# Moving the side work of a perceiver loop: three placement tables, a new order of 32 row maxima, and four small products of the last batch

## The chip, the cores and the metric

The kernel runs on one core of a Trainium2 chip. The metric is the device time of one execution in microseconds (us). The kernel before takes 948.94 us (median of 3 runs, 947.06 to 949.42). The profiled execution took 947.89 us, of which 946.2 us lie between its first and its last instruction (its span).

The engines are called by their names and, in rows, by their short forms: TensorE (PE; PEld is its weight load), VectorE (DVE), ScalarE (ACT), GpSimd (POOL), SyncE (SP; SPq rows are DMA instructions that it issues).

## The reference, cut to what matters

There are 16 batches. Each has 64 latent tokens and a context of 1601 tokens of 128 numbers. The first and largest layer is a cross attention with 16 heads; a small self attention and a mixture of experts follow on the 1024 latent tokens.

```python
x = layer_norm(image_embeds, ln1_g, ln1_b)      # 16 x 1601 x 128
l = layer_norm(latents, ln2_g, ln2_b)           # 16 x 64 x 128
q = l @ Wq
kv = concatenate([x, l], axis=1) @ Wkv
k, v = split(kv, 2)
w = einsum('bhqd,bhkd->bhqk', q * scale, k * scale)
w = softmax(w)                                  # over 1601 + 64 keys
out = einsum('bhqk,bhkd->bhqd', w, v) @ Wo
...
lam = exp(sum(lq1 * lk1, -1)) - exp(sum(lq2 * lk2, -1)) + 0.8   # in the self attention
```

## The kernel before, in words

**Slots and units.** The key and value maps are folded into the queries and the output map, so the attention works on the normalised tokens themselves. The loop has one slot per batch b, and a slot has 13 units (u = 0 to 12), one per tile of 128 context tokens; unit 12 holds the rest and the batch's own latents. Every number is kept as a high and a low float16 part, so each product is three matmuls in place of one. In each unit:

- TensorE computes the scores of tile u against 1024 query columns: six matmuls of 512 columns (lines 2142, 2145, 2151) into one half of the PSUM tile `S`. In the same unit it weighs tile u-2: six matmuls of 512 columns (2175, 2178, 2181) into `OA`. Scores of unit u wait for `lo_done` of unit u-2.
- ScalarE takes the exponential twice: as the high part (1859, `exponentials_high`) and in full precision back into `S` (1863, `exponentials_full`).
- VectorE subtracts the two and stores the low part (1539, `low_part`; "low" in the tables).

**Side work.** In the same slot the other steps of the batches around b are done, in the places that three tables give them. `TENSOR[u]` has two lists for TensorE: items ahead of the weighing of unit u, and items behind it. `VECTOR[u]` is VectorE's whole list for unit u. `SCALAR[u]` has three lists: ahead of the high exponential, between the two, and behind. Each engine works strictly in the order so written. The items are:

- `q` 0 to 3: the queries of batch b+1 (TensorE 2072 to 2074, 24 matmuls of 64 columns each; ScalarE copies the high part, 1845; VectorE stores the low part, 1518).
- `m` 0 to 31: the scores of batch b+1 with the high parts only, one block of 128 query columns by 512 (or, for the last column block c = 3, 65 + 64) keys each (2085, 2087, 2088). VectorE takes the row maximum of each block (1527), and at the end the maximum over all (1532). `M_ORDER` says which block comes when. `mt` and `shift` bring these maxima into the queries of b+1.
- `left_scores`, `left_sum`, `left_exp`, `left_low`, `left_turned`, `left_copy`, `left`: one context token that doesn't fit a tile, treated apart.
- `stat` (463, 13 a slot), `combine` (453 to 459) and `norm`: the layer norm of batch b+2. `split` 0 to 3 (1406): VectorE's high part of the tokens of batch b+1 in four groups; GpSimd follows each with the low part (1671).
- `outputs`, `latents`: the results of batch b-1 are copied out of PSUM. GpSimd then adds the denominators into `srow` (522). SyncE brings them into a column, `rcol` (512), VectorE takes the reciprocal (`inverse`, 787 and 789), SyncE writes it to memory and reads it back as `rb`, GpSimd multiplies, and ScalarE (`high`, 1840) and GpSimd split the product. `pj` 0 and 1 are the output projection of batch b-2 (2112 to 2114, 48 matmuls each).

**Two banks.** All side results of TensorE go to two PSUM banks, `WW` 0 and 1, in turn (`bank_of_items`). An item waits until the item before the last one, which used its bank, has been read (`bank_free`). The items `m` 5, `left_turned`, `q` 2, `q` 3, `m` 6, `m` 7 follow each other in this alternation: `q` 2 waits until `m` 5 has been reduced, and `m` 7 until the low part of `q` 3 has been stored.

**SyncE's order.** In each slot SyncE issues in this order, one after the other: the transpose of tiles 0 to 7 of b+1 (487), which waits for `split` 1; the transpose of the other tiles (489), which waits for `split` 3; the transpose of the low parts (491), which waits for GpSimd's last part; two small copies for the left token (498, 499); the load of the tokens of batch b+3, 768 KB and 32.5 KB (384, 386), in slots 0 to 12; then `rcol<-srow` (512), and what follows from it (515, 517), and at last `left_row` (507). All of them go through one queue.

**Last slot.** In slot 15 there is no batch to prepare. There the small weights' lambda of the self attention is computed: `small_weights_lambda` (VectorE 692 to 697), `lambdas_scalar` (ScalarE 706) and `lambdas_vector` (VectorE 701, 702), and TensorE starts the next layer in units 3 to 11.

Of the kernel before, what the change touches and what calls it, by code (L numbers as in the profile page):

```python
# [74 lines left out]
SHORT = [(r, 3) for r in range(8)]
M_ORDER = LONG[0:6]
for _k in range(8):
    M_ORDER += LONG[2 * _k + 6:2 * _k + 8] + SHORT[_k:_k + 1]
M_ORDER += LONG[22:24]
assert sorted(M_ORDER) == sorted(LONG + SHORT)  # L80
# [22 lines left out]
VECTOR = [("stat", "stat", "stat", "stat", "latents", "stat", "left_sum", "low", ("split", 0), ("split", 1), "stat", ("q", 0), ("split", 2), "stat",),  # L103
          ("low",),
          ("stat", "stat", "low", "stat", "left_low", ("split", 3), ("q", 1), ("m", 0), ("m", 1), "stat", ("m", 2), "stat", ("m", 3), "stat",),
          ("low", ("m", 4), ("m", 5),),
          ("combine", "low", ("q", 2), ("q", 3), ("m", 6),),
          ("low", ("m", 7), ("m", 8), "inverse", ("m", 9), ("m", 10),),
          ("low", ("m", 11), ("m", 12), ("m", 13),),
          ("low",),  # L110
          (("m", 14), ("m", 15), ("m", 16), ("m", 17), "low", ("m", 18), ("m", 19), ("m", 20), ("m", 21), ("m", 22),),
          ("low",),
          (("m", 23), ("m", 24), ("m", 25), ("m", 26), "low", ("m", 27), ("m", 28), ("m", 29), ("m", 30), ("m", 31),),
          ("low",),
          ("low",)]

SCALAR = [([], [], ["outputs"]),
          ([], [], [("q", 0)]),
          ([], [], ["projected", "left_exp", ("q", 1)]),
          ([], [], []),  # L120
          ([], [], []),
          (["left_copy"], [("q", 2), ("q", 3)], []),
# [2177 lines left out]
```

## Time and profile before

| what | value |
|---|---|
| median of 3 runs | 948.94 us (947.06 to 949.42) |
| profiled execution | 947.89 us, span 946.2 us |
| TensorE busy | 909.3 us, 96% of the span, 8268 matmuls |
| VectorE busy | 798.4 us, 84% |
| ScalarE busy | 701.2 us, 74% |
| GpSimd busy | 378.3 us, 40% |
| granted TensorE clock, mean | 0.994 |
| TensorE's share of the chain that ended last | 80% (VectorE 14%, ScalarE 3%) |

The busy time of a matmul runs from its start to its modelled end, 0.38 us for 512 columns, while the next one starts 0.215 us later; so TensorE can be called busy though it stands still for up to 0.16 us between two matmuls. Its idle time is therefore read from the starts of neighbouring matmuls in the timeline, not from the busy share.

### The profile page before, as it was taken

Reading aid. Unit: us, or ns where it says so; the run is one execution under the profiler, and the core shown is the slowest. Engines: PE = TensorE matmul, PEld = TensorE weight load, DVE = VectorE, ACT = ScalarE, POOL = GpSimd, SP = SyncE. Lnnn points to the kernel's source line nnn. Section 1 sums busy time; section 2 is a strip of 40 time slices with the busy share of each in tenths; the row PEclk is TensorE's granted clock in tenths of the full one; section 3 lists DMA queues with packets and bytes.
Section 4 is the critical chain, followed back from the end, with each engine's and each line's share of the span. In section 5 each row is a group of like instructions: output and inputs, shape, how many; then the busy total and the mean of one; then the engine's idle time right before and its main releaser. Section 6 shows DMA issues by size and latency. Waiting matters only on the chain.

```text
span 946.2 us, 20541 instructions
## 1 busy us (share of the span) xinstructions
PE 909.3 (96%) x8268; PEld 490.1 (52%) x8268; DVE 798.4 (84%) x1591; ACT 701.2 (74%) x1003; POOL 378.3 (40%) x378
## 2 busy tenths in 40 slices
PE   8679999999999999999999999999999999999996
PEld 5444445555454545454545454545454545566763
DVE  5979898979797979898989898888888786588987
ACT  4767878787878787878787878787879676755544
POOL 6472133343444343434343444343434231335345
PEclk9999999999999999999999999999999999999999
DMA  6402030303040303030303030303020200000000
GB/s 214 81 14 61 7 89 2 94 1 95 1 94 1 92 5 83 13 75 21 74 23 73 23 72 24 74 23 73 23 61 23 38 23 2 23 25 24 2 2 23
DMA packets 74566, 41.96 MB, mean 44 GB/s; under 512 B 62276, under 2 KB 69864, under 8 KB 74472
## 3 DMA queue, kind: packets, MB, share of 16 engines
q1 hardware_dynamic: 74184, 39.60, 16.8%
q8 instruction: 66, 1.08, 0.5%
q10 hardware_dynamic: 288, 1.05, 0.3%
q14 instruction: 28, 0.23, 0.1%
HBM read 25.98 MB, written 0.59 MB: 28 GB/s over the span
## 4 chain that ended last, share of the span: by engine, by line
PE 80%; DVE 14%; ACT 3%; issue 2%; DMA 1%; POOL 1%; POOLq 0%; DVEq 0%; ACTq 0%
PE S L2151 10%; PE S L2142 9%; PE OA L2175 9%; PE OA L2178 9%; PE OA L2181 9%; PE S L2145 9%; PE WW L2085 9%; PE WW L2112 1%; PE WW L2113 1%; DVE amx L803 1%; PE WW L2114 1%; PE WW L2072 1%; PE WW L2073 1%; PE WW L2074 1%; DVE mx L1510 1%
## 5 line engine op out<-in xcount | busy, mean ns | idle before, releaser
L1859 ACT ACTIVATE region<-S,sigma 128x1024 f16<-128x1024 f32 x208 | 231.6, 1113 | 135.9 <-PE S L2151 135.9
L1539 DVE TENSOR_TENSOR region<-S,region 128x1024 f16<-128x1024 f32 x208 | 252.4, 1214 | 42.3 <-ACT S L1863 42.3
L1527 DVE TENSOR_REDUCE mx<-WW 128x1 f32<-128x512 f32 (+1 forms) x480 | 262.7, 583 | 29.7 <-PE WW L2085 22.5
L1863 ACT ACTIVATE S<-S,sigma 128x1024 f32<-128x1024 f32 x208 | 224.4, 1079 | 0.0
L1671 POOL TENSOR_TENSOR xk<-raw,xk 128x508 f16<-128x508 f32 x64 | 63.2, 998 | 167.8 <-DVE xk L1406 167.8
L2142 PE MATMUL S<-region,xT 128*128 128x512 f16 (+1 forms) x416 | 124.5, 380 | 3.3 <-DVE region L1539 2.6
L2085 PE MATMUL WW<-xT,region 128*128 128x512 f16 x360 | 124.7, 380 | 3.0 <-DVE region L1518 2.1
L2175 PE MATMUL OA<-region,xk 128*128 128x512 f16 (+1 forms) x416 | 123.8, 379 | 0.0
L2145 PE MATMUL S<-region,xT 128*128 128x512 f16 (+1 forms) x416 | 123.7, 379 | 0.0
L2151 PE MATMUL S<-region,xT 128*128 128x512 f16 (+1 forms) x416 | 123.7, 379 | 0.0
L2178 PE MATMUL OA<-region,xk 128*128 128x512 f16 (+1 forms) x416 | 123.7, 379 | 0.0
L2181 PE MATMUL OA<-region,xk 128*128 128x512 f16 (+1 forms) x416 | 123.7, 379 | 0.0
L550 POOL TENSOR_TENSOR ew<-region,o_hi 128x1024 f16<-128x1024 f32 (+1 forms) x34 | 68.6, 2020 | 53.6 <-ACT o_hi L1840 53.6
L541 POOL TENSOR_TENSOR region<-region,rb 128x512 f32<-128x512 f32 x32 | 40.6, 1270 | 122.6 <-DMA rb<-inv_dram 122.6
L1797 ACT ACTIVATE raw<-raw,smc 128x128 f32<-128x128 f32 (+1 forms) x187 | 86.2, 486 | 0.0
L2151 PEld LDWEIGHTS S<-region,xT 128*128 128x128 f16 (+1 forms) x416 | 41.1, 99 | 48.6
L2178 PEld LDWEIGHTS OA<-region,xk 128*128 128x128 f16 (+1 forms) x416 | 40.6, 98 | 49.1
L2181 PEld LDWEIGHTS OA<-region,xk 128*128 128x128 f16 (+1 forms) x416 | 40.6, 98 | 49.1
L2145 PEld LDWEIGHTS S<-region,xT 128*128 128x128 f16 (+1 forms) x416 | 41.1, 99 | 46.8
L1660 POOL TENSOR_TENSOR smc<-smc,mhalf 128x13 f32<-128x13 f32 x16 | 39.0, 2434 | 61.8 <-DVE smc L459 61.8
L2085 PEld LDWEIGHTS WW<-xT,region 128*128 128x128 f16 x360 | 34.9, 97 | 54.0 <-DVE region L1518 14.1
L2142 PEld LDWEIGHTS S<-region,xT 128*128 128x128 f16 (+1 forms) x416 | 35.0, 98 | 43.5 <-issue 10.1
(318 smaller groups left out, 1830.2 us busy)
## 6 DMA issues: line engine op xcount, KB each, us to landing
raw<-ctx SPq DMA_DIRECT2D x16, 768.0 KB
rb<-inv_dram SPq DMA_DIRECT2D x16, 512.0 KB, 3.5
xT<-xk SPq DMA_TRANSPOSE x48, 3.1
left_row<-left_pT SPq DMA_DIRECT2D x48, 2.0 KB
raw<-ctx SPq DMA_DIRECT2D x16, 32.5 KB
WO_lo<-L_xattn_Wq ACTq DMA_DIRECT2D x1, 512.0 KB, 3.8
WO_hi<-L_xattn_Wkv ACTq DMA_DIRECT2D x1, 512.0 KB, 4.7
lx<-x SPq DMA_DIRECT2D x1, 512.0 KB, 5.7
```

The lines of the kernel that those rows point to most:

```text
L1527: nc.vector.tensor_reduce(mx[:, r, c:c + 1], W[BANK[("m", n)]][:, 0:width], AX.X, ALU.max)\
L1539: nc.vector.tensor_tensor(p_lo[k], src, p_hi[k], ALU.subtract).then_inc(lo_done.sem, 1)
L1797: ins = nc.scalar.activation(x_[0:r, t, :], x_[0:r, t, :], ACT.Identity, bias=smc[0:r, 2, t:t + 1], scale=smc[0:r, 1, t:t + 1])
L1859: nc.scalar.activation(p_hi[k], src, ACT.Exp, scale=sigma[:, 0:1])
L1863: nc.scalar.activation(src, src, ACT.Exp, scale=sigma[:, 0:1]).then_inc(e_done.sem, 1)
L2085: ins = mm(w, rows, xT_hi[p][:, 512 * c:512 * c + 512], start=True, stop=True)
L2142: mm(banks[r, k, :], hi, q_hi[p][:, cols(qc, k)], start=True, stop=False)
L2145: mm(banks[r, k, :], hi, q_lo[p][:, cols(qc, k)], start=False, stop=False)
L2151: ins = mm(banks[r, k, :], lo, q_hi[p][:, cols(qc, k)], start=False, stop=True)
L2175: mm(dst[k], hi, ph[r, cols[k]], start=first, stop=False)
L2178: mm(dst[k], hi, pl[r, cols[k]], start=False, stop=False)
L2181: ins = mm(dst[k], lo, ph[r, cols[k]], start=False, stop=last)
```

## The change

All three tables are written anew, and with them `M_ORDER`. The functions that carry out an item are the same. In words:

- The left token's steps come earlier: its exponential between the exponentials of unit 1, its low part on VectorE in `VECTOR[0]`.
- `pj` 1 moves from unit 2 to unit 1, and `q` 0 behind `pj` 0.
- ScalarE's `outputs` and several others go between the two exponentials or ahead of them; `high` 0 moves from unit 9 to the end of unit 7.
- On VectorE all four `split`s stand in `VECTOR[0]`, `inverse` moves from unit 5 to unit 3, `combine` from unit 4 to unit 5, and the maxima are spread in another way.
- The first parity of the bank alternation is turned (`(n + 1) % 2`).
- In the last slot lambda's steps move from units 0 to 2 to units 7 to 10 (`LAMBDA_AT = 7`).

```diff
-LONG = [(r, c) for c in range(3) for r in range(8)]
...
+M_ORDER = [(0, 0), (3, 0), (4, 0), (2, 0), (5, 0), (0, 1), (3, 1), (6, 0),
+           (0, 2), (2, 1), (7, 0), (4, 3), (6, 1), (3, 2), (6, 3), (4, 1),
...
-        ([("left_scores", 0), ("q", 0), ("pj", 0)], []),
-        ([("pj", 1), ("q", 1)], some(0, 1)),
-        (some(1, 1), some(2, 2)),
+        ([], [("left_scores", 0), ("pj", 0), ("q", 0), ("pj", 1)]),
+        ([("q", 1)], some(0, 1)),
+        (some(1, 2), some(3, 1)),
...
-          ("low", ("m", 7), ("m", 8), "inverse", ("m", 9), ("m", 10),),
+          ("stat", ("m", 1), ("m", 2), "stat", "low", ("m", 3), ("m", 4), "inverse", ("m", 5),),
...
-LEFT_AT = 9
+LEFT_AT = 8
...
-    banks = {item: n % 2 for n, item in enumerate(order)}
+    banks = {item: (n + 1) % 2 for n, item in enumerate(order)}
...
-                    if b is LAST and u == 0:
+                    if b is LAST and u == LAMBDA_AT:
                         small_weights_lambda(dve, link)
-                    if b is LAST and u == 2:
+                    if b is LAST and u == LAMBDA_AT + 3:
                         lambdas_vector(dve, link)
...
-                    if r % 4 == 0 and c in (0, 3):
-                        pe.wait_ge(q_hi_done.sem, q_hi_done.upto(turn, r // 4 + (2 if c == 3 else 0)))
...
+                    if k in Q_FIRST:
+                        pe.wait_ge(q_hi_done.sem, q_hi_done.upto(turn, Q_FIRST[k]))
+                    if k in Q_LATENTS:
+                        pe.wait_ge(q_hi_done.sem, q_hi_done.upto(turn, Q_LATENTS[k]))
```

The other lines of the three tables follow the same pattern. What they do to an engine's order is shown at three places. The first is VectorE in units 0 to 2 of a middle slot. `CAST xk<-raw` is a `split` (the one of 65 partitions is `split` 3), `BN_STATS` a `stat`, `region<-WW,region` the low part of queries, `region<-S,region` a `low`, `left_p` the left token's low part. Before:

```order
L1406 CAST xk<-raw 128x4x127
L463 BN_STATS stc<-raw 128x6
L1518 TENSOR_TENSOR region<-WW,region 128x512 [waits q_hi_done]
L1406 CAST xk<-raw 128x4x127
L463 BN_STATS stc<-raw 128x6
L1539 TENSOR_TENSOR region<-S,region 128x1024 [waits e_done]
L463 BN_STATS stc<-raw 128x6 x2
L1539 TENSOR_TENSOR region<-S,region 128x1024 [waits e_done]
L463 BN_STATS stc<-raw 128x6
L1548 TENSOR_TENSOR left_p<-left_e,left_p 128x8 [waits left_exp]
L1406 CAST xk<-raw 65x127
L1518 TENSOR_TENSOR region<-WW,region 128x512 [waits q_hi_done]
```

And now, from `split` 0 on (line numbers are 8 higher here):

```order
L1414 CAST xk<-raw 128x4x127 [waits pv_done,normed]
L1552 TENSOR_REDUCE left_s<-WW 128x8 [waits pe_left_scores]
L1547 TENSOR_TENSOR region<-S,region 128x1024 [waits e_done]
L1556 TENSOR_TENSOR left_p<-left_e,left_p 128x8 [waits left_exp]
L470 BN_STATS stc<-raw 128x6
L1414 CAST xk<-raw 128x4x127 x2
L470 BN_STATS stc<-raw 128x6 x3
L1526 TENSOR_TENSOR region<-WW,region 128x512 [waits q_hi_done]
L1414 CAST xk<-raw 65x127
L1547 TENSOR_TENSOR region<-S,region 128x1024 [waits e_done]
L1526 TENSOR_TENSOR region<-WW,region 128x512 [waits q_hi_done]
```

The last cast stood behind the `low`s of units 1 and 2; now it stands ahead of the `low` of unit 1, with two casts, three `stat`s and the low part of `q` 0 ahead of it.

The second place is VectorE around the reciprocal of the denominators (`rinv<-rcol`), which waits for the DMA of `rcol`. `mx<-WW` is a row maximum. Before, with `q` 2 and 3 at the head, in units 4 to 6:

```order
L1518 TENSOR_TENSOR region<-WW,region 128x512 [waits q_hi_done] x2
L1527 TENSOR_REDUCE mx<-WW 128x1 [waits pe_m]
L1539 TENSOR_TENSOR region<-S,region 128x1024 [waits e_done]
L1527 TENSOR_REDUCE mx<-WW 128x1 [waits pe_m] x2
L787 TENSOR_SCALAR rinv<-rcol 128x8 [waits den_col]
L789 RECIPROCAL rinv<-rinv 128x8 [waits den_scaled]
L1527 TENSOR_REDUCE mx<-WW 128x1 [waits pe_m] x2
```

Now, in units 3 and 4; the first `low` is that of unit 3:

```order
L1535 TENSOR_REDUCE mx<-WW 128x1 [waits pe_m] x2
L470 BN_STATS stc<-raw 65x6
L1547 TENSOR_TENSOR region<-S,region 128x1024 [waits e_done]
L1535 TENSOR_REDUCE mx<-WW 128x1 [waits pe_m] x2
L795 TENSOR_SCALAR rinv<-rcol 128x8 [waits den_col]
L797 RECIPROCAL rinv<-rinv 128x8 [waits den_scaled]
L1535 TENSOR_REDUCE mx<-WW 128x1 [waits pe_m]
L1547 TENSOR_TENSOR region<-S,region 128x1024 [waits e_done]
L460 TENSOR_TENSOR smc<-stc 128x13 [waits dve_step]
```

The reciprocal moved from behind `q` 2 and 3 and `m` 8 to between `m` 4 and `m` 5.

The third place is TensorE at the end of unit 4 and the start of unit 5, as it is now: `m` 5, the scores of unit 5, `left_turned` and the first matmul of `q` 2.

```order
L2095 MATMUL WW<-xT,region 128x512 [waits m_reduced]
L2152 MATMUL S<-region,xT 128x512 [waits lo_done]
L2152 MATMUL S<-region,xT 128x512
L2155 MATMUL S<-region,xT 128x512 x2
L2161 MATMUL S<-region,xT 128x512 x2
L2110 MATMUL WW<-ident,left_p 128x128 [waits left_low,m_reduced]
L2080 MATMUL WW<-cT_hi,G_hi 128x64 [waits m_reduced]
```

These seven rows are the same in the kernel before, but for the line numbers: on TensorE nothing moved here, and the last `m_reduced` is that of `m` 5 in both. SyncE's and GpSimd's orders are the same in both kernels throughout.

## Rows read from the trace of the kernel before

**Rows 1.** Busy time by stretch, slot 5: length, engines (count), granted clock, DMA

```profile
301.97:349.85 47.88, 47.85 (x430) 24.63 (x429) 41.60 (x81) 38.53 (x53) 19.01 (x17) 1.00 0.19 48
```

**Rows 2.** Timeline of TensorE, slot 5, units 3 and 5: start, length, what

```profile
314.35 0.59 PE L2151 MATMUL S<-region,xT 128*128 128x512 f16 x2
314.94 0.39 PE L2085 MATMUL WW<-xT,region 128*128 128x512 f16 x1
...
319.91 0.59 PE L2142 MATMUL S<-region,xT 128*128 128x512 f16 x2
...
321.26 0.19 PE L2072 MATMUL WW<-cT_hi,G_hi 128*128 128x64 f16 x1
321.29 0.19 PE L2073 MATMUL WW<-cT_lo,G_hi 128*128 128x64 f16 x1
```

**Rows 3.** Timeline of TensorE, slot 5, units 10 and 11

```profile
340.54 0.38 PE L2085 MATMUL WW<-xT,region 128*128 128x512 f16 x1
340.93 0.20 PE L2087 MATMUL WW<-xT,region 128*128 128x65 f16 x1
...
344.23 0.80 PE L2085 MATMUL WW<-xT,region 128*128 128x512 f16 x2
```

**Rows 4.** Timeline of ScalarE, slot 5, unit 0 (in brackets: idle before, releaser)

```profile
303.46 1.11 ACT L1859 ACTIVATE region<-S,sigma 128x1024 f16<-128x1024 f32 x1 [1.39 <-PE S L2151]
304.48 1.08 ACT L1863 ACTIVATE S<-S,sigma 128x1024 f32<-128x1024 f32 x1
```

**Rows 5.** Timeline of VectorE, slot 5, units 0 to 3

```profile
304.87 1.29 DVE L535 COPY region<-WW 128x512 f32<-128x512 f32 x2 [1.72 <-PE WW L2181]
...
306.75 1.21 DVE L1539 TENSOR_TENSOR region<-S,region 128x1024 f16<-128x1024 f32 x1
307.88 0.75 DVE L1406 CAST xk<-raw 128x508 f16<-128x508 f32 x2
...
309.64 1.40 DVE L1406 CAST xk<-raw 128x508 f16<-128x508 f32 x1
...
312.28 0.47 DVE L463 BATCH_NORM_STATS2 stc<-raw 128x6 f32<-128x128 f32 x2
...
314.07 0.21 DVE L1406 CAST xk<-raw 65x127 f16<-65x127 f32 x1
```

**Rows 6.** Timeline of GpSimd, slot 5, the low parts of the tokens

```profile
308.38 2.37 POOL L1671 TENSOR_TENSOR xk<-raw,xk 128x508 f16<-128x508 f32 x2 [8.91 <-DVE xk L1406]
311.12 1.15 POOL L1671 TENSOR_TENSOR xk<-raw,xk 128x508 f16<-128x508 f32 x1 [0.36 <-DVE xk L1406]
```

**Rows 7.** Timeline of SyncE, slot 5: DMA issues

```profile
314.31 1.20 SPq L489 DMA_TRANSPOSE xT<-xk  x1
...
319.55 0.56 SPq L512 DMA_DIRECT2D rcol<-srow  x1
```

**Rows 8.** Line 512 (`rcol<-srow`), all 16 slots: time from issue to landing

```profile
DMA to landing us min/median/max: 2.0/3.9/5.3
```

**Rows 9.** Timeline of VectorE, slot 5, units 4 to 6

```profile
319.60 1.27 DVE L1527 TENSOR_REDUCE mx<-WW 128x1 f32<-128x512 f32 x2
320.79 0.17 DVE L453 TENSOR_TENSOR smc<-stc 128x13 f32<-128x13 f32 x1
...
321.75 1.22 DVE L1539 TENSOR_TENSOR region<-S,region 128x1024 f16<-128x1024 f32 x1
323.22 1.29 DVE L1518 TENSOR_TENSOR region<-WW,region 128x512 f16<-128x512 f32 x2 [0.26 <-ACT region L1845]
...
326.95 0.16 DVE L787 TENSOR_SCALAR rinv<-rcol 128x8 f32<-128x8 f32 x1
327.15 0.20 DVE L789 RECIPROCAL rinv<-rinv 128x8 f32<-128x8 f32 x1
```

**Rows 10.** Timelines of VectorE and TensorE, slot 15 (the last), units 2 and 3

```profile
790.75 1.23 DVE L1539 TENSOR_TENSOR region<-S,region 128x1024 f16<-128x1024 f32 x1 [2.26 <-ACT S L1863]
...
792.03 0.60 PE L2142 MATMUL S<-region,xT 128*128 128x512 f16 x2 [0.91 <-DVE region L1539]
```

More of the change, by code:

```diff
@@ L70, with first_of @@
 MAXIMA = 32
-LONG = [(r, c) for c in range(3) for r in range(8)]
[L75 to L80, printed above, removed]
+M_ORDER = [(0, 0), (3, 0), (4, 0), (2, 0), (5, 0), (0, 1), (3, 1), (6, 0),
[3 rows of a table added]
+assert sorted(M_ORDER) == [(r, c) for r in range(8) for c in range(4)]
+def first_of(test):
+    return [test(r, c) for r, c in M_ORDER].index(True)
+Q_FIRST = {first_of(lambda r, c: r // 4 == k): k for k in range(2)}
+Q_LATENTS = {first_of(lambda r, c: c == 3 and r // 4 == k): 2 + k for k in range(2)}
+XT_FIRST, XT_SECOND = first_of(lambda r, c: c < 2), first_of(lambda r, c: c >= 2)
 def some(first, count):
@@ L101 @@
         ([("mt", 0), ("mt", 1)], [("weigh", 11)])]
-VECTOR = [("stat", "stat", "stat", "stat", "latents", "stat", "left_sum", "low", ("split", 0), ("split", 1), "stat", ("q", 0), ("split", 2), "stat",),
+VECTOR = [("stat", "stat", "stat", "stat", "stat", "latents", "stat", "stat", ("split", 0), "left_sum", "low", "left_low", "stat", ("split", 1), ("split", 2), "stat", "stat", "stat", ("q", 0), ("split", 3),),
           ("low",),
-          ("stat", "stat", "low", "stat", "left_low", ("split", 3), ("q", 1), ("m", 0), ("m", 1), "stat", ("m", 2), "stat", ("m", 3), "stat",),
-          ("low", ("m", 4), ("m", 5),),
-          ("combine", "low", ("q", 2), ("q", 3), ("m", 6),),
-          ("low", ("m", 7), ("m", 8), "inverse", ("m", 9), ("m", 10),),
-          ("low", ("m", 11), ("m", 12), ("m", 13),),
-          ("low",),
[L111 to L114, printed above, removed]
-          ("low",)]
@@ L117 @@
-SCALAR = [([], [], ["outputs"]),
-          ([], [], [("q", 0)]),
-          ([], [], ["projected", "left_exp", ("q", 1)]),
+          (("q", 1), ("m", 0), "low",),
+          ("stat", ("m", 1), ("m", 2), "stat", "low", ("m", 3), ("m", 4), "inverse", ("m", 5),),
+          ("low",),
+          ("combine", ("q", 2), ("q", 3), ("m", 6), ("m", 7), "low", ("m", 8), ("m", 9),),
+          (("m", 10), "low", ("m", 11),),
+          (("m", 12), ("m", 13), ("m", 14), "low", ("m", 15), ("m", 16), ("m", 17), ("m", 18),),
@@ new lines @@
+          ("low", ("m", 19), ("m", 20), ("m", 21),),
+          (("m", 22), "low", ("m", 23), ("m", 24),),
+          (("m", 25), ("m", 26), "low", ("m", 27), ("m", 28), ("m", 29),),
+          (("m", 30), ("m", 31), "low",),
+          ("low",)]
+SCALAR = [([], ["outputs"], []),
+          ([], ["left_exp"], []),
+          ([("q", 0), "projected"], [("q", 1)], []),
+          ([], [], []),
+          ([], [], ["left_copy"]),
+          ([("q", 2), ("q", 3)], [], []),
+          ([], [("norm", 0)], []),
+          ([("norm", 1)], [], [("high", 0)]),
+          ([("norm", 2), ("norm", 3)], [], [("norm", 4), ("norm", 5), ("norm", 6), ("norm", 7), ("norm", 8)]),
@@ L120 @@
           ([], [], []),
           ([], [], []),
[L122 to L130 removed]
+          ([("high", 1), ("norm", 9)], [("norm", 10)], [("norm", 11), ("norm", 12)]),
@@ L1906, in slot @@
                         act.wait_ge(wo_lo_done.sem, WO_GROUPS)
-                    if b is LAST and u == 1:
+                    if b is LAST and u == LAMBDA_AT + 1:
                         lambdas_scalar(act)
```

23 lines of the change are left out of this document (9 added, 14 removed), and 2 rows, old and new, of the table M_ORDER.

## The prediction

> **What bounds the kernel now.** I read the busy time by stretch first, then the timelines of each engine over one middle slot. Slot 5 runs from 301.97 to 349.85; times without a hundreds digit are from its start. It lasts 47.88 us, and TensorE is busy in 47.85 of them at full clock, with VectorE at 41.60, ScalarE at 38.53 [rows 1]. So TensorE bounds the loop, and the sum of matmuls is the same after the change: the most there is to win is TensorE's standing still. I read that from the starts. Two products of 512 columns start 0.21 apart (0.59 less 0.38) [rows 2], so the pair at 314.35 is over at 314.78, and the next starts at 314.94: 0.16 lost in unit 3, where `m` 1 waits for the low part of `q` 1. In unit 10 0.18 go the same way (340.54 and 0.21 against 340.93), and in unit 11 the pair at 344.23 takes 0.80 in place of 0.59 [rows 3]; with its neighbours that unit loses 0.44. Together 0.78 us a slot. All three are waits of a side product for its bank, that is for VectorE. What the tables change is worth 0.78 us at best in a slot, and has no upper limit the other way.
>
> **Units 0 to 4 on TensorE: minus 0.16.** `pj` 1 goes from unit 2 to unit 1 and `q` 0 behind `pj` 0, but the matmuls of units 0 to 4 together stay the same (`m` 0 to 5 in both), so unit 5 starts at 17.94 - 0.16 = 17.78 [rows 2]. The 0.16 go because `q` 1's low part is now first in `VECTOR[2]`, ahead of the `low` of that unit. `scores` of unit 3 needs the `low` of unit 1, which I put at 9.6 to 10.8, and starts at 11.5: covered, by 0.7.
>
> **The four casts, and what follows from the last.** VectorE copies the latents from 2.9 to 4.1 [rows 5]. ScalarE now copies the outputs ahead of its full exponential (each 1.0, an exponential starts 1.5 after the unit [rows 4]), so `low` 0 starts at 5.0 and, with the left token's two small exponentials behind it, `left_low` at 6.5. Then one `stat` (0.2), two casts (0.33 each), three `stat`s and the low part of `q` 0 (0.6) [rows 5, 9]: the last cast is reached at 6.5 + 0.2 + 0.7 + 0.6 + 0.6 = 8.5. GpSimd starts on the second group at 7.2 and does two groups in 2.37 [rows 6], until 9.5. In the trace the cast at 309.64, which begins while GpSimd works, takes 1.40 in place of 0.42 and ends 0.3 behind GpSimd's end at 310.75 [rows 5, 6]. So I take it that the last cast also waits until 9.5 and ends at 9.65; the other bound is 8.7, if it isn't held. Before it ended at 12.31 (314.07 and 0.21) [rows 5].
>
> SyncE's second transpose waits for this cast; `rcol<-srow` is issued 5.27 after the cast's end (319.55 against 314.28), with the transposes, the small copies and the load of the next tokens between, and it is SyncE's own issue time that fills these [rows 7]. GpSimd's `srow` follows the same cast and needs less. So `rcol` is issued at 14.9, 2.7 earlier than now, and lands 3.9 later by the median [rows 8], 4.0 in this slot: at 18.9.
>
> **The reciprocal: plus 0.9 and plus 0.37.** Now it stands in unit 6 at 24.98, when `rcol` has long landed [rows 9]. After the change it comes behind `m` 4 in unit 3's list. Unit 3 starts at 11.5; its exponentials start at 13.0 and 14.0 and end at 15.1 [rows 4]; `low` takes 1.13 until the next instruction [rows 5], `m` 3 and `m` 4 0.6 each [rows 9]: VectorE is there at 17.5, and waits 1.45 for `rcol`. Behind it in the queue are `m` 5, `low` 4, `combine`, the low parts of `q` 2 and 3, and `m` 6.
> TensorE wants `m` 5's bank for `q` 2 at 17.78 + 1.35 = 19.13 (321.26 less 319.91) [rows 2]. With `rcol` at 18.95, 0.33 for the two reciprocal rows and 0.69 + 0.06 for `m` 5 (length and release), `q` 2 starts at 20.03: 0.9 lost.
> A second loss is in the same unit. From `m` 5's start VectorE needs 0.6 + 1.13 (`low`) + 0.96 (`combine`, 320.79 to 321.75) + 0.6 + 0.69 + 0.06 = 4.04 until `q` 3's bank is free [rows 5, 9]. TensorE is ready for it with `m` 7 after 0.75 + 1.4 (`q` 2 and 3, 48 small matmuls at 0.029) + 1.3 (weighing) + 0.22 = 3.67 [rows 2]: 0.37 lost. Without the wait for `rcol`, `m` 5 starts 1.5 earlier and less than 0.1 of it is left.
>
> **Units 6 to 12: plus 0.35, minus 0.62.** By the same lengths every bank of units 6 to 10 is free in time, by 0.2 or more. In unit 11 `low` 10 stands ahead of `m` 27 and 28; the reduction of `m` 28 ends 3.3 after the unit's start, TensorE wants its bank at 3.1, and `m` 31 follows `m` 29 with another 0.15: 0.35 in place of the 0.62 of units 10 and 11 now. `high` 0 at the end of unit 7 (ScalarE, 30) needs GpSimd's product, which is done at about 27: covered by 3, and if it weren't, the exponential of unit 8 would stand behind it.
>
> **A middle slot** then takes 47.88 - 0.78 + 0.9 + 0.37 + 0.35 = 48.72, 0.84 more. The load ahead of `rcol` exists in slots 1 to 12, and the residual's load in its place in slot 13: 13 x 0.84 = +10.9. In slot 0 there is no reciprocal, in slot 14 no load, where `rcol` lands in 2.0 [rows 8] and so ahead of VectorE: there 0.35 is won in each, -0.7.
>
> **The last slot: minus 0.8.** In its unit 3 TensorE starts at 792.03 for want of `low` 1, which had waited 2.26 for ScalarE, and ScalarE for lambda's products [rows 10]: 1.07 lost, and 0.4 ahead of `pj` 0, whose bank is another now. Both go, -1.5. In units 7 and 8 ScalarE's small exponential waits for VectorE's products in the same way, 1.9 behind `low` 7, and holds the exponentials of unit 8 by 2.5. Scores of unit 10 have 1 us of slack on that, but the columns of the first layer's tile, copied behind them, come some 0.7 late for unit 9. Bounds are 0 and 2.5; I take 0.7, since the work behind is for the most part exponentials that have slack.
>
> **Sum.** +10.9 - 0.7 - 0.8 = +9.4 us on the profiled execution's 947.89: 957.3. The median of the runs is 1.05 above that execution, so 958.3.
>
> **Rivals.**
> *Faster: `rcol` is there in time.* It would have to land by 17.5, 2.6 after its issue. The least that the trace has is 2.0 [rows 8], and that speaks for it; the median of 3.9, and the load of 800 KB right ahead of it in the queue, against. Then the 0.9 and all but 0.08 of the 0.37 go: 15 slots x -0.35 = -5.3, with the last slot's -0.8 -6.1, 942.8. Chance 0.20, in which I also put what I may have wrong in VectorE's or SyncE's order of time.
> The Trainium skill (DMA: Bandwidth & Descriptors, on the two cost components) gives a DMA about 2.0 us plus its bytes at 436 GB/s. For 4 KB that is 2.0, which is this rival; line 512's own median of 3.9 doesn't agree, its least value does.
> *No change: the last cast slips in between two of GpSimd's instructions.* It then ends at 8.7, `rcol` lands at 18.0, VectorE waits 0.5 and `q` 2 isn't late, but `m` 7 still is, by 0.38: a slot takes 0.05 less than now, 13 x -0.05 - 0.7 - 0.8 = -2.2, 946.8. For it: the cast comes at 8.5, just behind the change of GpSimd's instructions at 8.4. Against: just behind. Chance 0.12.
> *Much slower: `rcol` lands as late as the longest of the rows, 5.3 after its issue, in most slots* [rows 8], because it and the load now meet the transposes of other data. Then 1.3 more a slot, 13 x 1.3 = 17: 975. For it the spread of the row, against it that the queue's order is the same. Chance 0.08.
> The forecast has 0.60.
>
> **How the numbers follow.** A difference of 0.3% (2.8 us) is about what a measurement of this kernel tells from none. Slower by more: 0.60 + 0.08 = 0.68; within: 0.12; faster: 0.20. The forecast's own range is 953 to 964 (0.4 a slot to either side of the landing, in 13 slots). For 8 in 10 it must reach down through the case of no change into the faster one, to 943, and up to 965; what is left out is the far side of the faster case and the much slower one.
>
> **What would show it.** In the changed kernel's trace: an idle time of VectorE ahead of the reciprocal, 1 to 2 us in slots 1 to 13, put down to the DMA of `rcol`; the start of `q` 2 on TensorE some 20 after the slot's start, behind a gap of about 0.9, and one of 0.4 ahead of `m` 7; the last cast lengthened to over 1 us; a slot of 48.7, but 47.5 for slot 14; no gap in unit 3; units 1 to 3 of the last slot without their 1.5. The prediction is wrong if `rcol` is issued ahead of 13.5 or lands within 2.6, or if VectorE reaches the reciprocal only at 19, since an earlier lateness would then have hidden it.

## The result and the profile after

The kernel after takes 964.19 us (median of 4 runs, 962.66 to 965.80) against 949.18 for the kernel before (4 runs, the three given above among them): a ratio of 1.0151, 95% interval 1.0129 to 1.0173. It is slower, as forecast (958.3, range 943 to 965), but by 15 us in place of 9.4, and only 0.8 below the upper end of that range. The profiled execution took 964.97 us, its span is 963.3.

From here on "middle slots" are slots 1 to 13, and the last slot is measured from its first scores to those of its unit 12. All numbers of this table are starts of TensorE's scores in the profiled executions. Lines of the kernel after are 7 to 10 higher than those of before (VectorE's `low` 1539 is 1547, the row maximum 1527 is 1535, `rcol` 512 is 519).

| stretch, us | before | after | forecast of the difference |
|---|---|---|---|
| ahead of the loop | 62.65 | 62.86 | 0 |
| slots 0 and 14 | 94.7 | 93.4 | -0.7 |
| middle slots | 623.3 | 636.3 | +10.9 |
| last slot, to unit 12 | 40.81 | 44.83 | -0.8 |
| the rest | 124.75 | 125.91 | 0 |

The spans differ by 17.1 where 9.4 were forecast; 4.8 of the 7.7 between them are in the last slot. The page's lines on the engines and on the chain that ended last:

```profile
PE 914.2 (95%) x8268; PEld 495.8 (51%) x8268; DVE 803.8 (83%) x1591; ACT 705.9 (73%) x1003; POOL 378.7 (39%) x378
...
PE 58%; DVE 21%; SPq 7%; DMA 5%; ACT 5%; issue 4%; POOL 0%; POOLq 0%; DVEq 0%; ACTq 0%
```

No engine does other work than before, yet TensorE's share of the chain fell from 80% to 58%. New on it are VectorE's casts, SyncE's issues (7%) and the DMA of `rcol` (5%): the chain from the last cast through the transposes to `rcol` now ends at something that TensorE waits for.

**A middle slot.** Slot 5 now runs from 303.00 to 351.62. Its windows row, with the columns of [rows 1] (length; busy time and count of TensorE, its weight load, VectorE, ScalarE and GpSimd; clock; DMA share; GB/s), answers to that:

```profile
303.00:351.62 48.62, 47.82 (x430) 24.73 (x429) 41.61 (x81) 38.77 (x53) 19.03 (x17) 1.00 0.19 47
```

Nearly the same busy times, full clock, 0.74 longer. Where it goes I follow along the chain, all in slot 5. First VectorE's timeline, units 0 and 4 (in brackets the idle time ahead and its releaser):

```profile
309.64 0.74 DVE L1414 CAST xk<-raw 128x508 f16<-128x508 f32 x2
...
311.47 1.10 DVE L1414 CAST xk<-raw 65x127 f16<-65x127 f32 x1
...
319.28 1.28 DVE L1535 TENSOR_REDUCE mx<-WW 128x1 f32<-128x512 f32 x2
321.83 0.17 DVE L795 TENSOR_SCALAR rinv<-rcol 128x8 f32<-128x8 f32 x1 [1.28 <-DMA rcol<-srow]
```

Then GpSimd's timeline beside the casts, and SyncE's issues:

```profile
310.12 2.37 POOL L1679 TENSOR_TENSOR xk<-raw,xk 128x508 f16<-128x508 f32 x2 [0.97 <-DVE xk L1414]
312.66 0.43 POOL L1679 TENSOR_TENSOR xk<-raw,xk 65x127 f16<-65x127 f32 x1 [0.16 <-DVE xk L1414]
```

```profile
312.61 1.20 SPq L496 DMA_TRANSPOSE xT<-xk  x1
...
318.63 0.56 SPq L519 DMA_DIRECT2D rcol<-srow  x1
```

The last cast takes 1.10 in place of the 0.21 of [rows 5], and ends just behind GpSimd's two groups, at 9.6 of the slot (they end at 9.5). `rcol` is issued at 15.6 and is there at 18.8, after a wait of 1.28. What TensorE makes of it:

```profile
322.07 0.22 PE L2110 MATMUL WW<-ident,left_p 128*128 128x128 f16 x1
322.86 0.20 PE L2080 MATMUL WW<-cT_hi,G_hi 128*128 128x64 f16 x1 [0.57 <-DVE mx L1535]
...
325.56 0.38 PE L2095 MATMUL WW<-xT,region 128*128 128x512 f16 x1
326.14 0.39 PE L2095 MATMUL WW<-xT,region 128*128 128x512 f16 x1 [0.20 <-DVE region L1526]
...
346.05 0.75 PE L2095 MATMUL WW<-xT,region 128*128 128x512 f16 x2
```

A matmul of 128 columns is a quarter of one of 512 and is followed after 0.06 where nothing is missing, so `q` 2's first matmul comes 0.73 late (322.86 less 322.07 and 0.06). `m` 7 comes 0.37 late (0.58 less 0.21). In [rows 2] `q` 2 starts 1.35 behind the scores, here 2.08. In unit 11 the pair of [rows 3] still takes 0.75 in place of 0.59, and the unit 3.95 as before.

Over all slots, from the view of line 519 (`rcol<-srow`): who waited for it (us, times), and its landing.

```profile
  DVE rinv L795: 18.2, 12
...
DMA to landing us min/median/max: 2.0/3.8/5.3
```

Slots 1 to 12 have the wait. In seven of them `rcol` is issued at 14.9 to 15.2 and lands 3.7 to 3.9 later; in slots 7 and 12 it lands 4.8 and 5.3 later. In slots 3, 5 and 10 it is issued at 15.6 to 15.8, and lands only 3.1 to 3.2 later: at 18.8 or 18.9 all the same. Slot 13 has no wait, since VectorE comes late to the reciprocal itself, but the slot is no shorter (48.69): in its unit 2 `m` 0 stands 1.0 for a transpose.

```profile
708.73 0.38 PE L2095 MATMUL WW<-xT,region 128*128 128x512 f16 x1 [0.96 <-DMA xT<-xk]
```

Slot 12 is the longest, 51.43: `rcol` lands 5.3 behind its issue, VectorE waits 2.77, and TensorE stands 2.06 ahead of `q` 2. From 667.05 on, within `q` 2's matmuls, the granted clock is half (1.2 in place of 2.4 GHz) for 3.4 us.

```profile
663.95 0.22 PE L2110 MATMUL WW<-ident,left_p 128*128 128x128 f16 x1
666.23 0.20 PE L2080 MATMUL WW<-cT_hi,G_hi 128*128 128x64 f16 x1 [2.06 <-DVE mx L1535]
```

**The last slot.** Its windows row, and three stretches of 4 us in its units 7 to 9 (columns as above):

```profile
792.56:837.39 44.83, 41.07 (x306) 21.55 (x306) 29.12 (x49) 32.02 (x39) 12.83 (x8) 0.96 0.04 13
816.00:820.00 4.00, 0.47 (x3) 0.00 (x0) 4.00 (x4) 2.27 (x3) 4.00 (x4) 1.00 0.00 0
820.00:824.00 4.00, 3.77 (x10) 1.43 (x11) 3.67 (x9) 0.35 (x2) 1.03 (x1) 0.58 0.00 0
824.00:828.00 4.00, 4.00 (x23) 2.27 (x22) 1.22 (x1) 3.62 (x5) 0.00 (x0) 0.99 0.00 0
```

TensorE stands for nearly the whole of the first stretch, VectorE is busy all through it. In the second one TensorE works again, but at a granted clock of 0.58 on the mean (3.4 us of it at 1.2 in place of 2.4 GHz), and 10 matmuls start in 4 us, where there would be 18 at 0.215 each. TensorE's and VectorE's timelines there:

```profile
815.88 0.59 PE L2191 MATMUL OA<-region,xk 128*128 128x512 f16 x2
820.23 0.66 PE L2152 MATMUL S<-region,xT 128*128 128x512 f16 x2 [3.76 <-DVE region L1547]
```

```profile
814.08 4.96 DVE L670 TENSOR_SCALAR raw<-raw,sm 128x128 f32<-128x128 f32 x4 [0.43 <-POOL sm L665]
818.96 1.21 DVE L1547 TENSOR_TENSOR region<-S,region 128x1024 f16<-128x1024 f32 x1
```

and GpSimd's:

```profile
814.02 1.25 POOL L548 TENSOR_TENSOR region<-region,rb 128x512 f32<-128x512 f32 x1
...
817.70 1.25 POOL L549 TENSOR_TENSOR region<-region,rb 128x512 f32<-128x512 f32 x1
```

Line 670 scales seven tiles of the next layer's tokens, four of them ahead of `low` 6, with one instruction each. In the kernel before the same four take 1.11, and GpSimd's products begin only behind them, since `rb` comes later. VectorE and GpSimd of the kernel before, at the same place of the program:

```profile
803.66 1.11 DVE L662 TENSOR_SCALAR raw<-raw,sm 128x128 f32<-128x128 f32 x4 [0.16 <-POOL sm L657]
```

```profile
808.47 1.27 POOL L541 TENSOR_TENSOR region<-region,rb 128x512 f32<-128x512 f32 x1 [4.84 <-DMA rb<-inv_dram]
...
812.15 1.28 POOL L542 TENSOR_TENSOR region<-region,rb 128x512 f32<-128x512 f32 x1
```

The starts of GpSimd's four products are 1.23 apart in both kernels (3.68 for three). So VectorE alone pays: each scaling, 0.28 before, waits for the end of one of GpSimd's instructions. Narrower windows of the kernel after show it one by one: the scalings start at 814.08, 815.29, 816.52 and 817.74, each 0.04 to 0.06 behind the start of a product, and each takes 1.28 to 1.30, to just behind that product's end. That is the reading which the experiments below test.

### The profile page after: what moved, and what is told of

Read it like the earlier page. It is cut to its first block, busy times and chain, and to the rows that moved or that the text cites. A ratio compares the mean times of both kernels' runs of the same rounds, so it can differ in the third digit from the quotient of the medians.

```text
span 963.3 us, 20541 instructions
## 1 busy us (share of the span) xinstructions
PE 914.2 (95%) x8268; PEld 495.8 (51%) x8268; DVE 803.8 (83%) x1591; ACT 705.9 (73%) x1003; POOL 378.7 (39%) x378
## 4 chain that ended last, share of the span: by engine, by line
PE 58%; DVE 21%; SPq 7%; DMA 5%; ACT 5%; issue 4%; POOL 0%; POOLq 0%; DVEq 0%; ACTq 0%
PE OA L2185 7%; PE S L2161 7%; PE OA L2188 7%; PE OA L2191 7%; PE WW L2095 7%; PE S L2152 7%; PE S L2155 6%; DMA rcol<-srow 5%; DVE region L1526 2%; DVE xk L1414 2%; SPq L498 2%; ACT S L1871 2%; DVE region L1547 2%; ACT region L1867 2%; DVE stc L470 2%
## 5 line engine op out<-in xcount | busy, mean ns | idle before, releaser
L2185 PE MATMUL OA<-region,xk 128*128 128x512 f16 (+1 forms) x416 | 124.8, 382 | 0.0
L1805 ACT ACTIVATE raw<-raw,smc 128x128 f32<-128x128 f32 (+1 forms) x187 | 82.4, 491 | 0.0
L2188 PEld LDWEIGHTS OA<-region,xk 128*128 128x128 f16 (+1 forms) x416 | 40.8, 98 | 49.8 <-issue 1.1
L2080 PE MATMUL WW<-cT_hi,G_hi 128*128 128x64 f16 x512 | 51.2, 195 | 10.4 <-DVE mx L1535 9.7
```

Source lines behind the costliest of these rows:

```text
L1805: ins = nc.scalar.activation(x_[0:r, t, :], x_[0:r, t, :], ACT.Identity, bias=smc[0:r, 2, t:t + 1], scale=smc[0:r, 1, t:t + 1])
L2185: mm(dst[k], hi, ph[r, cols[k]], start=first, stop=False)
L2188: mm(dst[k], hi, pl[r, cols[k]], start=False, stop=False)
```

## The experiments

Each is timed beside the kernel before; the ratio is to that. They ran in two groups of four (1 to 4 and 5 to 8) on two chips, on which the kernel before took 949.33 and 949.53. "Loop" is the time from the loop's first scores to those of slot 15.

| kernel | us | ratio (95%) | start | loop | last slot | rest |
|---|---|---|---|---|---|---|
| before | 949.2 | | 62.7 | 718.0 | 40.8 | 124.8 |
| after | 964.2 | 1.0151 | 62.9 | 729.7 | 44.8 | 125.9 |
| 1, reciprocal later | 952.2 | 1.0024 (1.0005 to 1.0043) | 65.0 | 717.2 | 43.5 | 124.7 |
| 2, `rcol` ahead of the load | 948.0 | 0.9980 (0.9965 to 0.9995) | 62.9 | 712.6 | 46.0 | 124.7 |
| 3, lambda early | 966.7 | 1.0164 (1.0134 to 1.0194) | 65.1 | 729.6 | 46.6 | 124.8 |
| 4, last reciprocal later | 965.1 | 1.0154 (1.0125 to 1.0183) | 64.6 | 729.4 | 44.8 | 124.8 |
| 5, last slot mended | 944.2 | 0.9933 (0.9915 to 0.9950) | 64.6 | 712.7 | 39.7 | 125.9 |
| 6, the same, lambda late | 943.3 | 0.9929 (0.9911 to 0.9947) | 62.7 | 713.0 | 40.0 | 125.8 |
| 7, the same, reciprocal early | 948.8 | 0.9993 (0.9978 to 1.0008) | 65.1 | 713.1 | 46.3 | 125.8 |
| 8, last cast ahead | 955.1 | 1.0062 (1.0039 to 1.0085) | 62.8 | 719.1 | 44.8 | 124.7 |

The four columns on the right are of one execution each. Start and rest differ by up to 2.4 and 1.2 between kernels that do the same there, with the granted clock: the start has a mean clock of 0.95 before, 0.89 after and 0.87 in experiment 1. The rest is 125.8 or 125.9 where the trace has a stretch of 3.4 us of half clock some 90 us behind the loop, and 124.7 or 124.8 where it has none; what brings that stretch is not shown.

### Experiment 1: the reciprocal one unit later

```diff
-          ("stat", ("m", 1), ("m", 2), "stat", "low", ("m", 3), ("m", 4), "inverse", ("m", 5),),
-          ("low",),
+          ("stat", ("m", 1), ("m", 2), "stat", "low", ("m", 3), ("m", 4), ("m", 5),),
+          ("low", "inverse"),
```

> The changed kernel with the reciprocal of the denominators moved by two places, from between m 4 and m 5 (end of VectorE's list of unit 3) to behind the low part of unit 4; nothing else. Theory (VectorE waits for rcol at the reciprocal, and m 5 behind it holds the bank of q 2): VectorE comes to the reciprocal at about 19.5 of a slot, when rcol has landed at 18.6 to 19.1 in most slots, so the gaps of unit 5 (0.73 and 0.37 in slot 5) go to under 0.1, a middle slot takes 47.5 in place of 48.6 to 48.9 on average, and the 13 slots give back some 18 us with the half-clock stretch of slot 12. In the last slot the denominators come back to GpSimd later, behind most of VectorE's normalisation, so most of the 3.9 us gap of unit 7 goes too. Expected 942 (939 to 946). Rival theory (the gaps of unit 5 come from ScalarE, which now copies q 2 and q 3 ahead of its exponential, or from the new spread of the maxima): the gaps stay, 960 to 964.

Measured 952.17. The loop falls from 729.7 to 717.2, less than before the change, and the middle slots from 636.3 to 623.8: 12.5 of the 13.0 lost there hang on VectorE's wait ahead of `m` 5. VectorE's row for the reciprocal in slot 5 (from 301.78 on) has no wait any more, at 19.7 of the slot.

```profile
321.49 0.16 DVE L795 TENSOR_SCALAR rinv<-rcol 128x8 f32<-128x8 f32 x1
```

The size was missed by 10: a slot takes 47.8 (of the gap at `m` 7 0.26 are left), the start is 2.3 longer than before at a lower clock, which was not foreseen, and the last slot stays 2.7 above that of before. Experiment 4 says why. The rival that puts the time elsewhere in the slot falls.

### Experiment 2: `rcol` issued ahead of the load

```diff
+                if b > 0:
+                    denominator_column(sp, Turn(b - 1))
                 if b + 3 < B:
                     load_raw(sp, Turn(b + 3))
...
                 if b > 0:
                     inverse_rows(sp, Turn(b - 1))
```

`denominator_column` is the wait for `srow` and line 519, taken out of `inverse_rows`. VectorE's order is that of the kernel after.

> The changed kernel with one thing changed in SyncE's order: rcol<-srow is issued ahead of the load of the next tokens (800 KB) in place of behind it; the reciprocal stays between m 4 and m 5. Theory: rcol is issued at about 13.9 of a slot and lands about 2 us later, at 16, ahead of VectorE's 17.5, so VectorE doesn't wait and a slot takes 47.5; the last slot has no load and keeps its 3.9 us gap in unit 7 and its half-clock stretch. Expected 946 (944 to 950). If the landing is late for another reason than the load ahead of it (the transposes' data, a fixed latency of 4 us), it lands at about 17.9 and VectorE still waits 0.4, q 2 is not late but m 7 is by 0.37: 951 to 954. Rival theory as before (ScalarE or the maxima): 964, unchanged.

Measured 947.95, within the range expected. SyncE's issues in slot 5 (from 298.42 on), VectorE's reciprocal, and the landing of all 16:

```profile
312.29 0.59 SPq L519 DMA_DIRECT2D rcol<-srow  x1
312.93 0.99 SPq L391 DMA_DIRECT2D raw<-ctx  x1
```

```profile
315.89 0.16 DVE L797 TENSOR_SCALAR rinv<-rcol 128x8 f32<-128x8 f32 x1
...
DMA to landing us min/median/max: 2.0/2.1/2.8
```

The same DMA, of the same 4 KB, lands 2.1 behind its issue in place of 3.8 (medians). The 1.7 are the load's, ahead of it in the same queue; the transposes are ahead of it in both kernels. With the issue 1.8 earlier (13.9 of the slot), `rcol` is there at 16, in slot 5 at 16.7, and VectorE gets to the reciprocal at 17.5 without a wait. The loop is 17.1 shorter than after and 5.4 shorter than before: what the tables were worth, once the wait is gone. The last slot, where SyncE has no load, stays long (46.0), and keeps the kernel from showing more than 0.2%.

The Trainium skill (DMA: Bandwidth & Descriptors, on the two cost components) gives a DMA of this size about 2.0 us, as a fit to DMAs that GpSimd issued. Experiment 2, where SyncE issues, agrees with 2.1; the kernel after with its 3.8 does not: here the sum holds only with no large load right in front.

### Experiment 3: lambda's products early in the last slot

```diff
-        LAMBDA_AT = 7
+        LAMBDA_AT = 1
```

> The changed kernel with lambda's products in units 1 to 4 of the last slot in place of units 7 to 10. Theory A (the last slot's 3.9 us gap in unit 7 comes from the port: GpSimd's normalisation, early now, makes VectorE's four and three scalings of the first layer's tiles four times as long, 1.28 in place of 0.34 each, and low 6 behind them is late; lambda has little part in it): the gap of unit 7 stays, 3.5 to 4, and units 2 and 3 get a gap of about 1 back; 964 to 966. Theory B (lambda's small exponential on ScalarE, which waits 5.4 us for VectorE in unit 8, is what holds TensorE): the gap of unit 7 and 8 goes, 959 to 961.

Measured 966.66, 0.7 above theory A's range, with 46.6 for the last slot: the late lambda is not what makes it long. Unit 7 takes 6.6 as in the kernel after. Units 1 to 3 take 10.46 as there: the gap of about 1 that was expected to come back in them did not, with lambda a unit later than in the kernel before. Lambda in unit 0, as before, was not tried. The 1.7 over the kernel after lie in unit 6 (0.6) and unit 8 (1.1, where the half clock lasts 6.8 us in place of 3.4).

### Experiment 4: the last slot's reciprocal behind `low` 4

```diff
-                        if item == "inverse" and post:
+                        if item == "inverse" and post and b is not LAST:
...
+                    if b is LAST and u == 4:
+                        reciprocals(dve, b.plus(-1))
```

> The changed kernel with the reciprocal moved behind the low part of unit 4 in the last slot alone; slots 1 to 14 as in the changed kernel. Theory A (port): GpSimd's four products of the denominators start at about 23.5 of the last slot in place of 21.5, by when VectorE has done four of its seven scalings at 0.34 each; the gap of unit 7 shrinks from 3.9 to under 1 and with it the half-clock stretch behind it goes (1.7 us); 959 (957 to 961), the middle slots unchanged at 48.9 on average. Theory B (lambda): unchanged, 964. With the first experiment it tells how much of that one's gain is the last slot's.

Measured 965.06, a miss by 6: the last slot is as long as after. Unit 7 has lost its gap (2.7 in place of 6.5), but unit 9 has one of 3.3 in its stead, and takes 9.4. GpSimd's and VectorE's timelines:

```profile
817.21 1.27 POOL L548 TENSOR_TENSOR region<-region,rb 128x512 f32<-128x512 f32 x1 [1.53 <-DMA rb<-inv_dram]
...
822.12 2.21 POOL L557 TENSOR_TENSOR ew<-region,o_hi 128x1024 f16<-128x1024 f32 x1
```

```profile
817.88 3.13 DVE L670 TENSOR_SCALAR raw<-raw,sm 128x128 f32<-128x128 f32 x3
820.93 1.21 DVE L1547 TENSOR_TENSOR region<-S,region 128x1024 f16<-128x1024 f32 x1
822.07 2.41 DVE L700 TENSOR_TENSOR lp<-lv 128x128 f32<-128x128 f32 x2
```

TensorE in unit 9:

```profile
828.12 2.08 PE L1114 MATMUL WW<-xk,wqkT 128*128 128x128 f32 x8 [3.15 <-ACT xk L659]
```

GpSimd's products come 1.8 us later than in the kernel after, and now meet the other three scalings (3.13 in place of 0.85 in the kernel before) and lambda's two products, which take 2.41 (0.48 in the kernel after) while GpSimd's line 557 runs. `low` 6, from PSUM, takes 1.21 as always. ScalarE's small exponential for lambda waits for all that, the copies of the first tile stand behind it, and TensorE waits for these in unit 9. The collision was moved, not removed. Experiment 1, whose last slot has the same order, shows the same: the three scalings take 3.29, and TensorE stands 3.16 in unit 9. Its slot is 1.3 shorter because the clock stays full behind that gap, where here it is half for 3.4 us. That alone neither confirms the reading nor refutes it, hence experiments 5 to 7.

### Experiment 5: experiment 2, and the last slot with the reciprocal in unit 5

```diff
-        LAMBDA_AT = 7
+        LAMBDA_AT = 1
...
+                    if b is LAST and u == 5:
+                        reciprocals(dve, b.plus(-1))
...
-                    if item[0] == "high" and post:
+                    if item[0] == "high" and post and not (b is LAST and item[1] == 0):
...
+                    if b is LAST and u == 9:
+                        outputs_high(b.plus(-1), 0)
```

> The kernel of the second experiment (rcol ahead of the load) with three things more, all in the last slot: the reciprocal stands in unit 5 again, the high part of the first half of the outputs (high 0) ahead of unit 9's exponential again, and lambda's products in units 1 to 4 of VectorE and ScalarE. Theory A (port: GpSimd's four products of the denominators and VectorE's scalings must not meet): the scalings take 0.34 each, TensorE has no gap over 0.2 in units 5 to 9, and the last slot up to its unit 12 takes 39.3 in place of 46.0, with the half-clock stretch gone: 941 (939 to 943), faster than the kernel before by 0.8%. Theory B (the last slot is slow for another reason, the new order of pj 1 in unit 1): it stays at 44 to 46, 946 to 948.

Measured 944.22 (941.71 to 944.82): faster than both kernels, 0.67% below before. The 3 us above the expectation lie in start and rest, which are 1.7 and 1.2 longer than in experiment 2, and 0.4 of them in the last slot. VectorE, GpSimd and the last slot's windows row:

```profile
799.21 1.11 DVE L672 TENSOR_SCALAR raw<-raw,sm 128x128 f32<-128x128 f32 x4 [0.16 <-POOL sm L667]
```

```profile
803.94 1.27 POOL L550 TENSOR_TENSOR region<-region,rb 128x512 f32<-128x512 f32 x1 [4.77 <-DMA rb<-inv_dram]
```

```profile
777.26:816.98 39.72, 39.44 (x306) 20.99 (x306) 24.62 (x49) 31.61 (x39) 12.88 (x8) 1.00 0.05 15
```

The products start behind the scalings as in the kernel before, the scalings take 1.11, and the slot is 1.1 shorter than before, at full clock.

### Experiment 6: experiment 5 with lambda at its late place

```diff
-        LAMBDA_AT = 1
+        LAMBDA_AT = 7
```

> As the fifth, but lambda's products stay where the change puts them, units 7 to 10 of the last slot. Tells lambda's own price with the scalings undisturbed. VectorE's first two products (two SBUF inputs) come at about 26, when GpSimd's products of the denominators start, and I expect one or both of them held to 1.3 or more in place of 0.2; ScalarE's small exponential waits for them to 28 or 29 and the columns of the first layer's tile behind it come 1 to 2.5 late for unit 9. Expected 942 to 944, 1 to 3 above the fifth. If lambda has no price there (ScalarE's slack covers it): as the fifth.

Measured 943.33 (942.81 to 943.41), within experiment 5's spread, where 1 to 3 more were expected. The last slot is 0.25 longer (39.97). That is a difference of two terms: with the late lambda unit 10 takes 4.11 in place of 3.49, and unit 6 takes 2.66 in place of 3.04. In unit 10 TensorE waits:

```profile
811.07 1.16 PE L1116 MATMUL WW<-xk,wqkT 128*128 128x128 f32 x8 [0.35 <-DVE Kx L807]
```

Lambda's two products were not held: they take 0.48, and GpSimd's start behind them. So the late lambda costs 0.6 in one unit, close to the 0.7 of the forecast, and gives 0.4 back in another.

### Experiment 7: experiment 5 with the last slot's reciprocal back in unit 3

```diff
-                        if item == "inverse" and post and b is not LAST:
+                        if item == "inverse" and post:
...
-                    if b is LAST and u == 5:
-                        reciprocals(dve, b.plus(-1))
```

> As the fifth, but the reciprocal of the last slot stays in unit 3, so that GpSimd's products come at 21.5 of the last slot. Port theory: VectorE's scalings are 1.28 each again, low 6 is late, and TensorE has a gap of 3.5 to 4 in unit 7, with a half-clock stretch behind it: 945 to 947, 4 to 6 above the fifth, though lambda is in units 1 to 4 and high 0 in unit 9. If the gap came from lambda or from high 0: as the fifth, 941.

Measured 948.76 (946.21 to 952.05), 4.5 above experiment 5; its profiled execution, the longest of ten, has 6.6 more in the last slot. GpSimd, VectorE and TensorE there, and the windows row:

```profile
800.26 1.26 POOL L550 TENSOR_TENSOR region<-region,rb 128x512 f32<-128x512 f32 x1
```

```profile
800.32 4.96 DVE L672 TENSOR_SCALAR raw<-raw,sm 128x128 f32<-128x128 f32 x4 [0.47 <-POOL sm L667]
```

```profile
806.46 1.04 PE L2159 MATMUL S<-region,xT 128*128 128x512 f16 x2 [3.80 <-DVE region L1552]
```

```profile
778.15:824.47 46.32, 42.01 (x308) 21.70 (x307) 28.28 (x49) 31.52 (x39) 12.89 (x8) 0.93 0.04 13
```

One instruction pair on VectorE stands two units earlier, lambda is early and `high` 0 late, and everything of the kernel after is back: the 4.96, TensorE's gap of 3.80, and behind it a clock of 0.5 (two matmuls in 1.04 in place of 0.59). That shows the cause in the last slot: it is the reciprocal's place. That it acts by way of GpSimd's products meeting the scalings is read from the rows, which agree in every kernel with the early reciprocal; no experiment took the products or the scalings away by themselves.

### Experiment 8: the last cast ahead of the `stat`s and `q` 0

```diff
-... ("split", 1), ("split", 2), "stat", "stat", "stat", ("q", 0), ("split", 3),),
+... ("split", 1), ("split", 2), ("split", 3), "stat", "stat", "stat", ("q", 0),),
```

> The changed kernel with one item of VectorE's list of unit 0 moved: the last cast (split 3) directly behind split 2, ahead of the three statistics and q 0's low part. It tests the step from the cast to rcol's landing. The cast comes at 7.3, when GpSimd has just begun its second group, and is held until about 8.35 in place of 9.5; it ends at 8.5. Then rcol is issued at 13.8 and lands at 17.6 to 18.0, VectorE waits 0.3 in place of 1.3, q 2 isn't late and m 7 is by 0.35: a middle slot of 47.85 in place of 48.7; the last slot is unchanged. Expected 949 to 951, no difference from the kernel before. If rcol's landing doesn't hang on this cast: slots as in the changed kernel, 964.

Measured 955.12, 9 below after, but 4 to 6 above what was expected. VectorE in slot 5 (from 300.21 on), and the sum of its waits for `rcol` over all slots with the landing:

```profile
306.84 1.83 DVE L1414 CAST xk<-raw 128x508 f16<-128x508 f32 x3
...
318.36 0.17 DVE L795 TENSOR_SCALAR rinv<-rcol 128x8 f32<-128x8 f32 x1 [0.60 <-DMA rcol<-srow]
```

```profile
  DVE rinv L795: 8.4, 12
...
DMA to landing us min/median/max: 2.0/3.8/4.6
```

The landing does hang on this cast: it ends at 8.5 in place of 9.6, and `rcol` is there 0.7 earlier in slot 5. The wait only halves, because SyncE's chain behind the cast stays 6 us long and the load stays ahead of `rcol`. Reordering VectorE wins back 10.6 of the loop's 11.7; reordering SyncE won 17.1.

## Why the prediction was right, and where it was wrong

- **What bounds the loop** held: TensorE's sum of matmuls is the same (47.82 busy in slot 5), and the difference lies in its gaps, none of it in work.
- **Units 0 to 4, minus 0.16**: no gap is left in unit 3.
- **The last cast**, predicted to be held until 9.65: 9.57 in slot 5. Its start at 8.5 was met too (8.47), but the terms written for it add up to 8.6. I had chosen this bound over 8.7, and the cast's 1.10 bears it out. The rival in which the cast slips in between two of GpSimd's instructions is refuted.
- **`rcol`**, predicted at 14.9 and 18.9: issued at 15.6 and there at 18.8 in slot 5, where the step from the cast to the issue took 6.1 in place of 5.27 and the landing 3.2 in place of 4.0. The two errors cancel there; in seven of the other eleven slots with the wait both terms hold. The median landing of 3.8 and 3.9 carried over from [rows 8]. The rival of the early landing, 2.0, is what experiment 2 shows once the load is no longer ahead.
- **The two gaps in unit 5**, 0.9 and 0.37: 0.73 and 0.37. **Unit 11**, 0.35: 0.44.
- **A middle slot** of 48.72: slot 5 took 48.62. But the 13 middle slots took 13.0 more in place of 10.9, since single slots are longer: slot 12 by 2.8 over slot 5 (the late landing, and 3.4 us of half clock). The step "13 x 0.84" took one slot for all, which leaves out the few whose landing lies at the far end of [rows 8]. It also counted slot 13 for the wait for `rcol`; that slot has no such wait, and is 0.8 longer for another cause, the transpose: that the count of 13 fits is luck. Slots 0 and 14 won 1.3 in place of 0.7.
- **The last slot, minus 0.8, is the step that failed**: it was plus 4.0. The part on units 1 to 3 was right: they take 10.46 in place of 11.97, the predicted -1.5. The part on units 7 and 8 named the wrong cause. It gave ScalarE's wait for lambda a price of 0.7 within 0 to 2.5; experiment 6 finds 0.6 in unit 10 (0.25 over the slot), and experiment 3 shows that the loss stays without it. What was overlooked is that `inverse` moves in the last slot's list too. For the middle slots I asked what the earlier reciprocal waits for; I did not ask what it releases. It releases `rb` and GpSimd's four products, and these then run beside VectorE's scalings: 3.85 more for four of them (4.96 less 1.11). That gives a gap of 3.9 on TensorE, and 1.7 more by the half clock behind it. My own reading of the held cast in [rows 5, 6] was the same effect, with its price of about one GpSimd instruction each.
- **The rest**, forecast at nothing: +1.2 after the last slot and +0.2 ahead of the loop. Both vary that much between kernels that are alike there (table above), with the stretches of half clock, so I count them to the spread of executions.
- **The number.** The direction and the wait for `rcol` in the middle slots came as forecast. That 964.19 lies within 943 to 965 is owed to the width of the range: the forecast's own range was 953 to 964, and a term of +4 was missing from it.

By stretch: 0.2 + 13.0 - 1.3 + 4.0 + 1.2 = 17.1, which is 963.3 less 946.2.

What stays open: why slot 13's transpose lands 1 us late, and unit 11's 0.44, which no experiment addressed. The late transpose is no chance event: TensorE waits for it in all eight experiments (0.9 to 1.2). In the kernel after and in experiments 1, 2, 5 and 8 an 8 KB transfer of the queue that loads instructions took 1.7 to 2.0 us just then, in the kernel before 0.42, at another place of the slot. That it is the cause was not tested.

## What to carry to other kernels

When a step is moved earlier, follow it both ways: up to the transfer that it waits for, with what stands ahead of that transfer in its queue, and down to the work that it releases on other engines, and what that will now run beside. Do it once for every stage that uses the same table, first and last slots above all. A small transfer on the critical path belongs ahead of a large one in its queue: that exchange of two issues took 17 us off the loop of the kernel after, where VectorE waits for the small one. In the kernel before nothing waits for it, and the exchange alone was not tried there; against that kernel, new tables and exchange together are worth 5.4 in the loop.

## What the runs showed of the hardware that was not expected

- **VectorE behind GpSimd, instruction by instruction.** A scaling of 128 x 128 float32 from and to SBUF takes 1.11 for four alone and 4.96 for four beside GpSimd's products, which are not slowed (1.23 apart in both). It is held once per instruction, for about the length of one of GpSimd's, so four short instructions pay four times (experiment 7 repeats 4.96). Casts are held too (0.21 to 1.10), and a product of two SBUF inputs (0.48 to 2.41 for two). A `low` with PSUM input beside the same work takes 1.21, as always. The Trainium skill (SBUF — State Buffer, on who interferes with whom) says that the two engines share a pair of ports as an exclusive lock, that casts and `tensor_scalar` can take it, that a `tensor_tensor` with both inputs in SBUF contends with GpSimd's reads, and that who issues first blocks the other for the whole instruction. The trace agrees on which of VectorE's instructions are held, and that each is held to the end of one of GpSimd's, by the numbers just given. The other direction, GpSimd held by VectorE, hardly shows: its products keep their 1.23, and its line 557 takes 2.21 beside lambda's two products in place of some 2.13.
- **The clock around a standstill.** In the last slot TensorE stands 3.75 to 3.81 us in unit 7 in the kernel after and in experiments 2, 3, 7 and 8. The granted clock there is half for 3.4 us (kernel after, experiment 8) or 6.8 us (experiments 2, 3 and 7, where it falls before the standstill ends). Unit 8 takes 5.48 in the first two and 6.3 to 6.7 in the others, in place of the 3.80 of experiment 5; so such a gap is paid for about 1.4 to 1.7 times. The length of the gap alone does not decide it: around a gap of 2.06 in slot 12 of the kernel after and one of 3.15 in experiment 4's unit 9 the clock fell for 3.4 us, around one of 3.16 in experiment 1's unit 9 and one of 1.91 in slot 12 of experiment 4 it did not.
- **A load in front.** A DMA of 4 KB landed 2.1 us behind its issue (2.8 at most), and 3.8 (5.3 at most) with 800 KB issued right ahead of it on the same queue. Where it was issued 0.8 later behind the same load, it landed at the same time of the slot.
